# A transformer block pair on one core: the first self-attention stores its outputs by feature, and the dense stage behind it divides them by the softmax sums

## The chip, the cores and the metric

One Trainium2 chip, one of its cores. The metric is the device time of one launch, in microseconds (us), lower is better. The engines of the core are TensorE (PE, with its weight loads as PEld), VectorE (DVE), ScalarE (ACT), GpSimd (POOL) and SyncE (SP, which here issues DMAs).

## What is computed

Two cross-attention transformer layers run in sequence over x of 8 samples x 512 tokens x 320 features, with a context of 8 x 64 tokens x 192 features. There are 20 heads of 16 features. Each layer, in float32:

```python
x = x + attn(ln(x), ln(x), q1, k1, v1) @ o1_w + o1_b     # self-attention
x = x + attn(ln(x), ctx,   q2, k2, v2) @ o2_w + o2_b     # cross-attention
x = x + (a * gelu(g)) @ ff_w2 + ff_b2                    # a, g = split(ln(x) @ ff_w1 + ff_b1)

# attn, per sample and head:
sim = q @ k.T * 16 ** -0.5
out = softmax(sim) @ v
```

The second layer also rounds q, k, v and the softmax weights to 8-bit steps. The change concerns the self-attention of the first layer and the dense stage behind it.

## The kernel before

The launch is a chain of stages, each a block of its own: all engines must have ended one before the next begins. In the first layer they are a dense stage (layer norm, q, k, v), `self_attention` (here some 250 to 700 us from the start of the span), a dense stage that projects the attention output, adds it to x, normalises and makes q2 (`dense_phase` with main "q", about 702 to 840 us), `cross_attention`, and a feed-forward stage. The second layer has the same sequence with other attention functions.

`self_attention` works in 40 rounds, one for each quad (4 heads of one sample; 5 quads a sample), with work of three quads in flight. In round n, each of 8 units j makes two tiles of natural scores of quad n+2 (`nat`, in three PSUM banks; DVE takes the row maximum of each, L1391), two transposed tiles of scores of quad n (`sT`, two double banks; ACT takes the exponentials into `probs`, L1325) and a part of the product of `probs` with the values of quad n-1 into `o_ps` (L1277). In unit 1 the row maxima of the next quad are transposed on PE (L1267), and ACT copies them (L1330). `sT` is also lent to this and to the turn of the output, so each unit waits for the bank used two steps before. The values have 32 columns a head (VCOL): 16 of v, one of ones, which makes the softmax sum, and 15 of zeros. So `o_ps` holds for 4 heads 32 rows each, by feature: 16 outputs, the sum in row 16, and zeros.

At the start of round n ACT copies `o_ps` of quad n-2 to `o_sb` (L1318). In unit 2, `turn_output` transposes it by four PE transposes into `sT` (L1287), ACT copies that to `o_turned` (L1334), DVE takes the reciprocal of its sums (L1385), POOL multiplies (L1352), and SP stores 256-byte rows of 4 x 16 outputs by token into `self_out` (L1232). SP also issues all loads, in the order of its code.

The dense stage runs its samples through a written order, `body`, the same for all engines; a step of `ahead` a works on sample b+a in round b. The steps of the attention output are `oT` (transpose 128 columns of `attn_nat` on PE, L848; ACT rounds it to `oT_hi`, L949; DVE makes the rest `oT_lo`, L1012), and `oproj` (8 matmuls, L326, then DVE adds to x, L1016). `stats` is the layer norm's statistics (L1023 to L1028, POOL's power at L804), `norm` is z (L1034), `zT` its transpose with two ACT passes and `hT_lo` on DVE (L961, L963, L1048), and q the product that is stored as a high and a low part (L984, L1070). SP loads `attn_nat` of sample b+3 after the last `oT` transposes of sample b+2 (L691, L695):

```python
body = [("stats", 0), *oT[0:2], items[0], oT[2], ("norm", 0), items[1], items[2], oproj[0], ("double", 0),
        zT[0], zT[1], oproj[1], zT[2], oproj[2], oproj[3]]
```

The dense stages of the second layer take their attention output by feature already (`by_feature`), and do without the transposes.

## Time and profile before

| | |
|---|---|
| time of 3 runs, us | 3338.16, 3343.64 (median), 3344.39 |
| time of the profiled execution, us | 3342.7 |
| its span, us | 3341.0 |
| mean granted TensorE clock over the span, share of full speed | 0.841 |
| busy share of the span: PE, DVE, ACT, POOL | 88%, 65%, 57%, 24% |

The busy share of PE counts matmuls from issue to their modelled end; they are pipelined, so it is not its share of peak. The shares are means over stages with different limits, so a stage that is changed has to be read by itself. A granted clock of 1.00 is 2.4 GHz, 0.50 is 1.2 GHz.

### The profile page before, as it was taken

To read this page: it belongs to the slowest core of one execution; us is meant where nothing else is said; L and a number is where in the kernel's file an instruction comes from. 1 tells how busy PE (TensorE), PEld (TensorE's weight loads), DVE (VectorE), ACT (ScalarE), POOL (GpSimd) and SP (SyncE) were. 2 spreads that over 40 slices of the span, in tenths; PEclk is the share of its full clock that TensorE was granted. 3 is DMA by queue.
4 is the path that set the end of the run, shared out by engine and by line. 5 is a ranking of instruction groups with operands and counts; after the bars stand their busy time and mean duration, and the time that the engine had idled before them with its cause. 6 is when DMAs were issued, how large, how long until landed. Compare 5 with 4: busy or idle time off the path is not lost. (4 is left out here: it accounts for less than half of the span.)

```text
span 3341.0 us, 47964 instructions
## 1 busy us (share of the span) xinstructions
PE 2936.9 (88%) x15594; PEld 1775.7 (53%) x15594; DVE 2157.7 (65%) x3834; ACT 1892.4 (57%) x3214; POOL 805.5 (24%) x1149
## 2 busy tenths in 40 slices
PE   6989999978696999998959999879978577899999
PEld 5754444457455888886731111111126342788888
DVE  5668888837453444444649999968868685444443
ACT  4328888844353232233549999989975355333322
POOL 2021221114640000000027888200003471200000
PEclk9969999989798999998975555555559898899999
DMA  8663333336762000001567557266723213010000
GB/s 228 211 166 101 106 107 103 90 80 158 165 176 46 10 10 19 9 0 38 152 173 163 128 137 164 32 90 83 97 56 96 79 45 92 26 36 18 25 17 16
DMA packets 358243, 296.57 MB, mean 89 GB/s; under 512 B 175602, under 2 KB 281914, under 8 KB 358058
## 3 DMA queue, kind: packets, MB, share of 16 engines
q1 hardware_dynamic: 347994, 273.93, 34.0%
q0 software_dynamic: 7280, 18.07, 2.1%
q10 hardware_dynamic: 2784, 2.29, 0.4%
q8 instruction: 94, 1.54, 0.2%
q14 instruction: 91, 0.75, 0.1%
HBM read 177.53 MB, written 114.52 MB: 87 GB/s over the span
## 5 line engine op out<-in xcount | busy, mean ns | idle before, releaser
L1591 PE MATMUL nat<-k_stack,q_stack 48*128 48x512 bf16 x640 | 381.0, 605 | 71.5 <-DMA k_stack<-k1w 31.1
L1391 DVE TENSOR_REDUCE neg_max<-nat 128x1 f32<-128x512 f32 x640 | 400.7, 682 | 61.3 <-PE nat L1250 61.2
L1625 DVE TENSOR_REDUCE m_all<-nat 128x1 f32<-128x512 f32 x640 | 423.3, 691 | 18.1 <-PE nat L1591 17.8
L804 POOL TENSOR_TENSOR rstd<-var_eps,neghalf 128x4 f32<-128x4 f32 x48 | 51.9, 1081 | 1588.0 <-DVE var_eps L1028 1588.0
L1645 ACT ACTIVATE nat<-nat,m_all 128x512 f32<-128x512 f32 x640 | 427.7, 2130 | 3.0 <-DVE m_all L1625 2.9
L1645 ACT ACTIVATION_READ_ACCUMULATOR nat<-nat,m_all 128x1 f32 x640 | 403.6, 1674 | 0.0
L1054 DVE SCALAR_TENSOR_TENSOR ff<-outp,bias,gel 128x512 f32<-128x512 f32 x160 | 120.1, 751 | 417.6 <-PE outp L326 417.6
L1325 ACT ACTIVATE probs<-sT 128x1024 f32<-128x1024 f32 x320 | 328.0, 1027 | 93.1 <-PE sT L1259 85.5
L968 ACT ACTIVATE gel<-outp,bias 128x512 f32<-128x512 f32 x160 | 110.0, 688 | 351.6 <-PE outp L326 351.6
L1839 ACT ACTIVATE exps<-sT 128x1024 f32<-128x1024 f32 x320 | 293.4, 1573 | 10.5 <-PE sT L1788 10.5
L972 ACT CAST ff_hi<-ff 128x512 fp32r<-128x512 f32 x160 | 99.2, 620 | 312.3 <-DVE ff L1054 312.3
L1591 PEld LDWEIGHTS nat<-k_stack,q_stack 48*128 48x128 bf16 x640 | 64.1, 102 | 387.9 <-ACT nat L1645 350.8
L1876 DVE TENSOR_SCALAR probs<-exps 128x1024 bf16<-128x1024 f32 x320 | 218.3, 692 | 67.8 <-ACT exps L1839 67.8
L1788 PE MATMUL sT<-q_stack,k_stack 51*128 51x512 bf16 x640 | 194.2, 604 | 34.6 <-DMA q_stack<-shift_rows 12.2
L1250 PE MATMUL nat<-k_stack,q_stack 48*128 48x512 f32 x640 | 200.8, 524 | 20.1 <-DMA k_stack<-k_hi 11.7
L1277 PE MATMUL o_ps<-probs,v_stack 128*32 128x256 f32 x2560 | 199.8, 394 | 1.1 <-issue 1.1
L1057 DVE TENSOR_TENSOR ff_lo<-ff,ff_hi 128x512 fp32r<-128x512 f32 x160 | 122.1, 763 | 109.7 <-ACT ff_hi L972 109.7
L1048 DVE TENSOR_TENSOR hT_lo<-h,hT_hi 128x512 fp32r<-128x512 f32 x144 | 111.6, 780 | 106.0 <-ACT hT_hi L963 105.7
L1250 PEld LDWEIGHTS nat<-k_stack,q_stack 48*128 48x128 f32 x640 | 80.0, 193 | 163.6 <-DVE neg_max L1391 129.2
L1259 PE MATMUL sT<-q_stack,k_stack 51*128 51x512 f32 x640 | 157.7, 430 | 0.5 <-ACT probs L1325 0.2
L1788 PEld LDWEIGHTS sT<-q_stack,k_stack 51*128 51x128 bf16 x640 | 34.0, 102 | 184.0 <-ACT exps L1839 165.7
L326 PE MATMUL outp<-hT_hi,Wff_hi 128*128 128x512 f32 x320 | 125.9, 393 | 4.6 <-DVE hT_lo L1048 4.6
(561 smaller groups left out, 7163.3 us busy)
## 6 DMA issues: line engine op xcount, KB each, us to landing
v<-vpad SPq DMA_DIRECT2D x64, 320.0 KB, 2.8
q_stack<-q_part SPq DMA_DIRECT2D x90, 160.0 KB, 5.8
k_stack<-k1w SPq DMA_DIRECT2D x90, 160.0 KB, 10.5
q_stack<-q_hi SPq DMA_DIRECT2D x160, 64.0 KB, 2.5
v_stack<-v SPq DMA_DIRECT2D x40, 256.0 KB, 3.2
q_stack<-q_hi SPq DMA_DIRECT2D x80, 128.0 KB, 2.8
raw<-v SPq DMA_DIRECT2D x16, 640.0 KB, 14.9
k_stack<-k_hi SPq DMA_DIRECT2D x158, 64.0 KB, 2.2
```

The costliest lines, as they stand in the source:

```text
L326: mm = pe.matmul(out, stay, move, start=(n == 0), stop=(n == len(terms) - 1))
L1250: pe.matmul(nat[(16 * n + t) % 3][:, :], q_stack[half, n % RING, pr, qt * P:(qt + 1) * P], k_stack[half, n % RING, pr, :], start=True, sto ...
L1259: mm = pe.matmul(sT[use % 2][:, ab, :], k_stack[half, n % RING, pr, kt * P:(kt + 1) * P], q_stack[half, n % RING, pr, :], start=True, stop ...
L1277: mm = pe.matmul(o_ps[VCOL * h:VCOL * h + VCOL, tok], v_stack[:, n % 2, kt, VCOL * h:VCOL * h + VCOL], probs[:, n % 2, h, kt, tok], start= ...
L1325: act.activation(probs[:, n % 2, 2 * pr:2 * pr + 2, kt, :], sT[use % 2][:, :, :], ACT.Exp, scale=DH ** -0.5).then_inc(s["a_turn_free"], 1)
L1391: dve.tensor_reduce(neg_max[:, n % 2, qt, 2 * pr + ab:2 * pr + ab + 1], nat[(16 * (n + 2) + t) % 3][:, :], AX.X, ALU.max, negate=True).the ...
L1591: pe.matmul(bank[i % NAT][:, :], q_stack[half, slot, g, pr, qt * P:(qt + 1) * P], k_stack[half, slot, g, pr, :], start=True, stop=True).th ...
L1625: dve.tensor_reduce(k.m_all[:, column(i // TILES, i % TILES)], bank[i % NAT][:, :], AX.X, ALU.max, negate=True).then_inc(s["e_max_ready"], 1)
L1645: act.activation(b[:, :], b[:, :], ACT.Exp, bias=k.m_all[:, col], accum_out=k.s_all[:, col]).then_inc(s["a_nat_free"], 1)
L1788: mm = pe.matmul(sT[u % TURNS][:, ab, :], k_stack[half, slot, g, pr, kt * P:(kt + 1) * P], q_stack[half, slot, g, pr, :], start=True, stop ...
L1839: act.activation(exps[:, u % EXPS], sT[u % TURNS][:, :, :], ACT.Exp).then_inc(s["a_turn_free"], 1)
L1876: dve.tensor_scalar(probs[:, u % KEPT], exps[:, u % EXPS], ROUND, -ROUND, ALU.add, ALU.add).then_inc(s["e_rounded"], 1)
```

## The change

`self_attention` no longer turns its output. `o_sb` is doubled, and SP stores it as it is: 128 rows (4 heads x 32) of 512 tokens, 2 KB each, for every quad. When the five quads of a sample are stored, SP loads the 20 rows of sums back as 80 x 128 values, DVE takes one reciprocal for the sample (`invert`, in the middle of the maxima of a later round), POOL splits it into a rounded high part and the rest (`split_shares`), and SP stores both into a new scratch, `self_shares`. All of it is some rounds behind the quads; for the last sample it follows the last quad.

The dense stage loads per sample the 40 rows of shares (20 high, 20 low) and the outputs by feature (four DMAs). Its `oT` transposes go. In a new step `scale`, of the third sample ahead and late in the round, a matmul of the 40 rows with a constant 0/1 matrix (`spread`) puts the share of each head on its 16 feature rows in a bank of the old `oT` ring, and DVE multiplies `attn_T` by that bank in place, three times a sample. ACT and DVE then make `oT_hi` and `oT_lo` of the next sample from SBUF. SP loads sample b+3 when DVE has made the last `oT_lo` of sample b+2.

```diff
+            if scale:
+                ahead["scale"] = 3
             body = [("stats", 0), *oT[0:2], items[0], oT[2], ("norm", 0), items[1], items[2], oproj[0], ("double", 0),
-                    zT[0], zT[1], oproj[1], zT[2], oproj[2], oproj[3]]
+                    zT[0], zT[1], oproj[1], zT[2], *scale[0:2], oproj[2], *scale[2:], oproj[3]]
         else:
             ahead = {"stats": 1, "norm": 1, "zT": 1}
...
+                        heads = rows(attn_in, b * (QUADS * P), QUADS * P).rearrange("(h c) t -> h c t", c=VCOL)[:, 0:DH, :]
+                        loads = [(attn, heads)]
+                        if main == "ff":
+                            shared = rows(recips, b * HEADS, HEADS).unsqueeze(1).broadcast_to([HEADS, DH, TOK])
+                            loads.append((shares, shared))
+                        else:
+                            sp.dma_start(words(shares[:, :]), rows(recips, b * (2 * HEADS), 2 * HEADS)
+                                         ).then_inc(s["attn_in_loaded"], 16)
+                        for tile, src in loads:
+                            for c in range(2):
+                                sp.dma_start(tile[:, c, :], src[8 * c:8 * c + 8]).then_inc(s["attn_in_loaded"], 16)
+                            for half in range(2):
+                                sp.dma_start(tile[64 * half:64 * half + 64, 2, :], src[16:HEADS]
+                                             ).then_inc(s["attn_in_loaded"], 16)
+                        return
                     src = rows(attn_in, b * D, D)
...
+                    if kind == "scale" and main != "ff":
+                        if isinstance(b, int) and b + m == 0:
+                            pe.wait_ge(s["spread_set"], at["spread_set"] + 1)
+                        if m == 0:
+                            pe.wait_ge(s["attn_in_loaded"],
+                                       at["attn_in_loaded"] + b * (16 * n_attn) + 16 * n_attn)
+                        bank_free(pe, st, b)
+                        pe.matmul(bank_of(st, r)[:, :], spread[:, m * P:(m + 1) * P], shares[:, :], start=True, stop=True
+                                  ).then_inc(s[turned[st][0] + "_full"], 1)
...
-                    if kind == "oT":
+                    if kind == "scale":
+                        if m == 0:
+                            dve.wait_ge(s["attn_in_loaded"],
+                                        at["attn_in_loaded"] + b * (16 * n_attn) + 16 * n_attn)
+                        share, done = shares[:, m, :] if main == "ff" else bank_of(st, r)[:, :], "o_scaled"
+                        if main != "ff":
+                            done = turned[st][0] + "_drained"
+                            bank_full(dve, st, b)
+                        dve.tensor_tensor(attn[:, m, :], attn[:, m, :], share, ALU.mult).then_inc(s[done], 1)
...
+                def load_sums(b):
+                    for r in range(2):
+                        wait(sp, f"a_o_stored{r}", 16 * ((QUADS * (b + 1) - r + 1) // 2))
+                    sums_of = rows(out, b * (QUADS * P), QUADS * P).rearrange("(h c) t -> h c t", c=VCOL)[:, DH, :]
+                    sp.dma_start(sums[:, :], sums_of.rearrange("h (x t) -> h x t", t=P)
+                                 ).then_inc(s["a_sums_loaded"], 16)
+
+                def store_shares(b):
+                    wait(sp, "a_share_split", 2 * b + 2)
+                    for i, half in enumerate((share_hi, share_lo)):
+                        sp.dma_start(rows(recips, (2 * b + i) * HEADS, HEADS).rearrange("h (x t) -> h x t", t=P),
+                                     words(half[:, :])).then_inc(s["a_recip_stored"], 16)
...
                         load(n + AHEAD, k_stack, kk, (0, 1, 0))
-                    if exists(n - 3):
-                        wait(sp, "a_o_normed", n - 2)
-                        sp.dma_start(rows(out, (n - 3) * TOK, TOK).rearrange("(t p) c -> p t c", p=P),
-                                     o_nat[:, (n - 3) % 2].rearrange("p t h c -> p t (h c)")
-                                     ).then_inc(s[f"a_o_stored{(n - 3) % 2}"], 16)
+                    if exists(n - 2):
+                        wait(sp, "a_o_copied", n - 1)
+                        sp.dma_start(rows(out, (n - 2) * P, P), o_sb[:, n % 2, :]).then_inc(s[f"a_o_stored{n % 2}"], 16)
+                    if exists(n - 3) and (n - 3) % QUADS == QUADS - 1:
+                        load_sums((n - 3) // QUADS)
+                    if exists(n - 6) and (n - 6) % QUADS == QUADS - 1:
+                        store_shares((n - 6) // QUADS)
...
-                def turn_output(n):
-                    wait(pe, "a_o_copied", n + 1)
-                    wait(pe, "a_turn_free", output_use(n) - 1)
-                    for qt in range(TT):
-                        mm = pe.transpose(output_bank(n)[:, qt * P:(qt + 1) * P], o_sb[:, qt * P:(qt + 1) * P],
-                                          k.ident[:, :])
-                    mm.then_inc(s["a_turn_full"], 1)
 
...
-                        if exists(n - 2) and j == 2:
-                            turn_output(n - 2)
                         for i in PRODUCTS.get(j, ()) if exists(n - 1) else ():
...
-                        wait(act, "a_turn_full", output_use(n - 3) + 1 if n > 2 else 0)
-                        act.copy(o_sb[:, :], o_ps[:, :]).then_inc(s["a_o_copied"], 1)
+                        wait(act, f"a_o_stored{n % 2}", 16 * (n // 2 - 1))
+                        act.copy(o_sb[:, n % 2, :], o_ps[:, :]).then_inc(s["a_o_copied"], 1)
                     for j in range(UNITS):
...
-                        if exists(n - 2) and j == 2:
-                            wait(act, "a_turn_full", output_use(n - 2) + 1)
-                            wait(act, "a_o_normed", n - 3)
-                            act.copy(o_turned[:, n % 2, :], output_bank(n - 2)).then_inc(s["a_turn_free"], 1)
...
+                def split_shares(b):
+                    wait(pool, "a_recip", b + 1)
+                    wait(pool, "a_recip_stored", 32 * b)
+                    pool.tensor_copy(share_hi[:, :], shares[:, :]).then_inc(s["a_share_split"], 1)
+                    wait(pool, "a_share_split", 2 * b + 1)
+                    pool.tensor_tensor(share_lo[:, :], shares[:, :], share_hi[:, :].bitcast(F32), ALU.subtract
+                                       ).then_inc(s["a_share_split"], 1)
...
-                    if n >= 4:
-                        norm(n - 4)
+                    if n > 2 * QUADS and n % QUADS == 1:
+                        split_shares(n // QUADS - 2)
...
-                for n in range(-2, NQ + 3):
-                    if exists(n - 3):
-                        wait(dve, "a_turn_free", output_use(n - 3) + 1)
-                        wait(dve, "a_o_normed", n - 4)
-                        o = o_turned[:, (n - 3) % 2, :].rearrange("p (t h c) -> p t h c", t=TT, h=4)
-                        dve.reciprocal(recip[:, (n - 3) % 2], o[:, :, :, DH]).then_inc(s["a_recip"], 1)
+                def invert(b):
+                    wait(dve, "a_sums_loaded", 16 * (b + 1))
+                    wait(dve, "a_share_split", 2 * b)
+                    dve.reciprocal(shares[:, :], sums[:, :]).then_inc(s["a_recip"], 1)
+
+                for n in range(-2, NQ + 4):
+                    if not exists(n + 2) and exists(n - 4) and (n - 4) % QUADS == QUADS - 1:
+                        invert((n - 4) // QUADS)
...
+                        if t == 8 and exists(n - 4) and (n - 4) % QUADS == QUADS - 1:
+                            invert((n - 4) // QUADS)
...
-                        next_weights=[w1])
+                        next_weights=[w1], by_feature=True, recips=self_shares)
```

Two places in the order of instructions. First PE in `self_attention`, units 1 to 3 of one round. Before, with the line numbers of the kernel before (`o_ps` x4 are the products of one step of quad n-1; `nat` and `sT` are the score tiles):

```order
L1250 MATMUL nat_174<-k_stack,q_stack 128x512
L1250 MATMUL nat_172<-k_stack,q_stack 128x512
L1259 MATMUL sT_175<-q_stack,k_stack 128x512 x2
L1267 MATMUL sT_176<-identb,parts 32x128 x4
L1277 MATMUL o_ps<-probs,v_stack 32x256 x4
L1250 MATMUL nat_173<-k_stack,q_stack 128x512
L1250 MATMUL nat_174<-k_stack,q_stack 128x512
L1259 MATMUL sT_175<-q_stack,k_stack 128x512 x2
L1287 MATMUL sT_176<-ident,o_sb 128x128 x4
L1277 MATMUL o_ps<-probs,v_stack 32x256 x4
L1250 MATMUL nat_172<-k_stack,q_stack 128x512
L1250 MATMUL nat_173<-k_stack,q_stack 128x512
```

The same place in the changed kernel:

```order
L1314 MATMUL nat_176<-k_stack,q_stack 128x512
L1314 MATMUL nat_177<-k_stack,q_stack 128x512
L1323 MATMUL sT_179<-q_stack,k_stack 128x512 x2
L1331 MATMUL sT_178<-identb,parts 32x128 x4
L1341 MATMUL o_ps<-probs,v_stack 32x256 x4
L1314 MATMUL nat_175<-k_stack,q_stack 128x512
L1314 MATMUL nat_176<-k_stack,q_stack 128x512
L1323 MATMUL sT_179<-q_stack,k_stack 128x512 x2
L1341 MATMUL o_ps<-probs,v_stack 32x256 x4
L1314 MATMUL nat_177<-k_stack,q_stack 128x512
L1314 MATMUL nat_175<-k_stack,q_stack 128x512
```

The four transposes of `o_sb` are gone, and the two `sT` banks simply alternate from there on.

Second, DVE in the dense stage at the end of a round, from the second `oproj` on (the register rows compute what a semaphore is compared with). Before:

```order
L1016 TENSOR_TENSOR x_resid<-x_resid,oproj_225 128x320
L1047 REGISTER_ALU
L1048 TENSOR_TENSOR hT_lo<-h_214,hT_hi 128x512
L635 REGISTER_ALU
L1016 ISA
L1016 TENSOR_TENSOR x_resid<-x_resid,oproj_224 128x320
L635 REGISTER_ALU
L1016 ISA
L1016 TENSOR_TENSOR x_resid<-x_resid,oproj_225 128x320
L115 REGISTER_ALU
L1023 BN_STATS bn<-x_resid 128x6 x4
```

In the changed kernel, from the last `hT_lo` on:

```order
L1104 TENSOR_TENSOR hT_lo<-h_219,hT_hi 128x512
L1056 ISA
L644 ISA
L1062 TENSOR_TENSOR attn_T<-attn_T,oT_234 128x512
L644 REGISTER_ALU
L1062 TENSOR_TENSOR attn_T<-attn_T,oT_233 128x512
L644 REGISTER_ALU
L1072 ISA
L1072 TENSOR_TENSOR x_resid<-x_resid,oproj_229 128x320
L644 REGISTER_ALU
L1062 TENSOR_TENSOR attn_T<-attn_T,oT_234 128x512
```

Three multiplications have come in ahead of the last two additions to x, and so ahead of the next statistics.

## Rows read from the trace of the kernel before

**Rows 1.** The page's first line: the span.
```profile
span 3341.0 us, 47964 instructions
```

**Rows 2.** Windows: stretch, its length, busy us (x instructions) by engine, clock, DMA.
```profile
260.00:690.00 430.00, 417.64 (x3857) 175.39 (x3856) 359.83 (x606) 353.58 (x409) 79.87 (x210) 1.00 0.36 99
740.00:800.00 60.00, 52.57 (x312) 43.44 (x310) 47.60 (x103) 30.77 (x51) 25.87 (x35) 1.00 0.70 173
2540.00:2600.00 60.00, 55.07 (x305) 43.69 (x304) 52.11 (x110) 35.39 (x57) 20.46 (x9) 1.00 0.34 107
```

**Rows 3.** Timeline of one self-attention round: start, duration, engine, line, work, [idle before].
```profile
464.33 0.50 PE L1250 MATMUL nat<-k_stack,q_stack 48*128 48x512 f32 x2
...
465.19 0.42 PEld L1287 LDWEIGHTS sT<-ident,o_sb 128*128 128x128 f32 x4 [0.33 <-issue]
...
465.78 0.64 PE L1277 MATMUL o_ps<-probs,v_stack 128*32 128x256 f32 x8
...
466.35 0.50 PE L1250 MATMUL nat<-k_stack,q_stack 48*128 48x512 f32 x2
...
466.88 2.51 DVE L1391 TENSOR_REDUCE neg_max<-nat 128x1 f32<-128x512 f32 x4 [0.72 <-PE nat L1250]
...
467.58 0.56 PE L1250 MATMUL nat<-k_stack,q_stack 48*128 48x512 f32 x2
```

**Rows 4.** Copies and reciprocals of the self-attention: counts, durations (ns), first and last start.
```profile
L1318 ACT COPY o_sb<-o_ps x40: 578/580/586, 253.6 to 696.4; 128x512 f32<-128x512 f32 x40
L1385 DVE RECIPROCAL recip<-o_turned x40: 242/244/255, 265.2 to 698.4; 128x16 f32<-128x16 f32 x40
```

**Rows 5.** Timeline of ACT, second and third copy of the rounds.
```profile
265.19 0.58 ACT L1318 COPY o_sb<-o_ps 128x512 f32<-128x512 f32 x1
...
276.76 0.58 ACT L1318 COPY o_sb<-o_ps 128x512 f32<-128x512 f32 x1
```

**Rows 6.** Timeline of SP's queue, the end of one round.
```profile
470.68 0.42 SPq L1232 DMA_DIRECT2D self_out<-o_nat  x1
473.19 0.39 SPq L1237 DMA_DIRECT2D v_stack<-v  x1
```

**Rows 7.** Timeline between the two stages.
```profile
696.41 0.59 ACT L1318 COPY o_sb<-o_ps 128x512 f32<-128x512 f32 x1 [2.60 <-PE o_ps L1277]
...
698.75 0.62 POOL L1352 TENSOR_TENSOR o_nat<-o_turned,recip 128x256 f32<-128x256 f32 x1 [3.90 <-issue]
701.84 2.09 SPq L691 DMA_DIRECT2D attn_nat<-self_out  x4
...
707.40 1.57 PEld L848 LDWEIGHTS oT<-ident,attn_nat 128*128 128x128 f32 x8 [9.93 <-DMA attn_nat<-self_out]
```

**Rows 8.** DMAs that write or read o_nat, from issue to landing.
```profile
DMA to landing us min/median/max: 2.0/2.1/4.1
```

**Rows 9.** Timeline of one dense round: DVE, and SP's load.
```profile
766.12 1.68 DVE L1023 BATCH_NORM_STATS2 bn<-x_resid 128x6 f32 x4 [0.26 <-DVE x_resid L1016]
...
768.49 1.29 DVE L1012 TENSOR_TENSOR oT_lo<-oT,oT_hi 128x512 fp32r<-128x512 f32 x2
...
770.08 3.01 SPq L691 DMA_DIRECT2D attn_nat<-self_out  x4
...
771.15 2.66 DVE L1034 TENSOR_SCALAR z<-x_resid,mv,rstd 128x320 f32 x4
...
776.79 0.69 DVE L1048 TENSOR_TENSOR hT_lo<-h,hT_hi 128x512 fp32r<-128x512 f32 x1 [1.39 <-ACT hT_hi L963]
...
779.46 0.69 DVE L1048 TENSOR_TENSOR hT_lo<-h,hT_hi 128x512 fp32r<-128x512 f32 x1 [0.25 <-ACT hT_hi L963]
...
781.50 0.89 DVE L1023 BATCH_NORM_STATS2 bn<-x_resid 128x6 f32 x2
```

**Rows 10.** The second layer's dense stage of the same kind, by feature: DVE.
```profile
2553.05 1.51 DVE L1034 TENSOR_SCALAR z<-x_resid,mv,rstd 128x320 f32 x4
...
2556.94 2.43 DVE L1048 TENSOR_TENSOR hT_lo<-h,hT_hi 128x512 fp32r<-128x512 f32 x2 [0.81 <-ACT hT_hi L963]
```

More of the change, by code:

```diff
@@ L523, in dense_phase @@
         has_o = wo is not None
+        scale = [("scale", m) for m in range(3)] if recips is not None else []
         oT, oproj, zT = ([(x, m) for m in range(n)] for x, n in (("oT", 3), ("oproj", TT), ("zT", 3)))
@@ L529, in dense_phase @@
         if main == "ff":
-            ahead = {"oT": 1, "oproj": 1, "stats": 1, "norm": 1, "zT": 1, "tail": -1}
-            between = [[("tail", 0)], oT[0:2], oT[2:], oproj[0:2], oproj[2:], [("stats", 0)], [("norm", 0)],
+            ahead = {"oT": 1, "oproj": 1, "stats": 1, "norm": 1, "zT": 1, "tail": -1, "scale": 1}
+            between = [[("tail", 0), *scale], oT[0:2], oT[2:], oproj[0:2], oproj[2:], [("stats", 0)], [("norm", 0)],
                        zT[0:2], zT[2:], []]
@@ L551, in dense_phase @@
                 turned = {st: x for st, x in turned.items() if st[0] != "oT"}
+                turned.update({st: ("oT", st[1], 3) for st in scale})
             if not has_o:
@@ L940, in step @@
                             bank_full(act, st, b)
+                        elif scale and main == "ff":
+                            act.wait_ge(s["o_scaled"], at["o_scaled"] + b * 3 + m + 1)
+                        elif scale:
+                            name, count = bank_read(scale[m], b)
+                            act.wait_ge(s[name], count)
                         elif m == 0:
@@ L1220, in _ @@
                 load(1, k_stack, kk, (0, 1, 0))
-                for n in range(-2, NQ + 3):
+                for n in range(-2, NQ + 6):
                     if exists(n + AHEAD):
@@ L1239, in _ @@
                                      ).then_inc(s[f"a_v_loaded{(n + 1) % 2}"], 16)
-                for r in range(2):
-                    wait(sp, f"a_o_stored{r}", 16 * (NQ // 2))
+                wait(sp, "a_recip_stored", 32 * BATCH)
             @block.tensor
```

61 lines of the change are left out of this document (31 added, 30 removed).

## The prediction

> **What bounds the kernel now.** I read the page first. The span is 3341.0 us [rows 1], but its stages have different limits, so I cut it with the view of windows at the two stages that the change touches. In the self-attention PE is busy 417.6 of 430 us, DVE 359.8, ACT 353.6, at a granted clock of 1.00 [rows 2]. PE is the bound there, with DVE not far behind. In the dense stage behind it PE is busy 52.6 of 60 us and DVE 47.6 [rows 2]: near each other, so what a round costs has to be read from the order of the work.
>
> The timeline of one self-attention round shows what the removed turn costs. The two score tiles of unit 2 start at 464.33, the transposes' weight loads at 465.19, the products behind them at 465.78, and the tiles of unit 3 at 466.35; unit 3, which has no turn, ends at 467.58 [rows 3]. So unit 2 takes 2.02 us and unit 3 takes 1.23. DVE stands idle 0.72 us in that place, waiting for PE [rows 3].
>
> In the dense stage the reader is to follow DVE round the loop. From one `bn` (766.12) to the next (781.50) is 15.38 us. The first half goes to the end of z (771.15 + 2.66 = 773.81), 7.69 us, in which DVE has hardly a gap. In the second half, also 7.69 us, it waits for ACT's two passes over each `zT` tile: `hT_lo` of the first tile comes at 776.79 after 1.39 us idle, that of the third at 779.46 [rows 9].
>
> **The self-attention, round by round.** Off PE go four transposes a quad. From the first weight load of them to the next products is 0.59 us (465.78 - 465.19), the least that this saves. Unit 2 less unit 3 is 0.79 us, the most. DVE can follow by its idle 0.72. I take 0.62, near the lower end: part of the difference of the units is that the transposed scores of unit 2 wait for exponentials, and that wait stays. Rounds with a turn at the full pace are 38 (the last two quads are turned when no new scores are made), so 38 x 0.62 = 23.6 us; the bounds are 22.4 and 30.0. In the last full round of products one more turn goes, 0.6.
>
> ACT loses a copy a round (0.58 us, by the other copy of that shape [rows 4]) and POOL a product; neither is the bound, I count nothing. DVE loses a reciprocal of 0.24 us a quad [rows 4]. The trace has a round without it, because the first quad's reciprocal came only at 265.2: from the copy at 253.6 to that at 265.19 is 11.6 us, and the next, with a reciprocal, is 11.57 [rows 4, 5]. So it is worth nothing, and the eight larger ones that come in (one a sample, set in the middle of the maxima, where PE's longest unit leaves DVE a gap) I count at nothing too; uncovered they would be 8 x 0.3 = 2.4.
>
> SP's queue: the store of 256-byte rows becomes one of 2 KB rows, 0.42 us to issue as before, I assume; one quad in five adds a load, one in five two stores, 0.4 each. After its store SP is done at 471.10 and issues the values at 473.19, when the products have ended: 2.1 us of slack a round [rows 6]. A round that is 0.62 shorter and has up to 0.8 more to issue still leaves 0.7. The new waits on SP are for things some rounds old, except `a_o_copied`, which is signalled at the start of the same round, ahead of the shift that SP has waited for already.
>
> **Between the stages.** Before, the last copy of `o_ps` starts at 696.41 and the next stage's first load at 701.84, 5.4 us later [rows 7]. Now behind that copy stand, one after another: the copy with its signal 0.7, the store to its landing 2.1 [rows 8], the load of the sums 2.3 (an estimate from the same row), a reciprocal 0.4, two POOL operations 0.4 each (between nothing and the 0.62 of [rows 7], for half the elements a partition) with 0.2 between, two stores 0.4 + 2.1, the block's end 0.3. That is 9.3, and with 0.1 for each of four hand-overs 9.7: +4.2 us, between +3 and +6.
>
> **The dense stage, round by round.** Off PE go 12 transposes a sample, and three matmuls come in. DVE gets three products of 128x512 out of PSUM, which the trace does not show as such. The nearest row is the pair of `oT_lo`, one operand in PSUM, 1.29 us for two of 0.69, so 0.60 from one to the next [rows 9]. 0.69 if nothing overlaps is the upper end; nothing excludes that ACT's waits hide them, so zero is the lower.
>
> Where do they lie? They stand behind the last `hT_lo`, ahead of the last two additions to x, and the next `bn` waits for those. First half of a round: 7.5 (7.69 less the small gap before the third `oT_lo`, which waited for a transpose). Second half: in this stage the first `hT_lo` comes 2.98 us after z's end, in the second layer's, which has no transposes, 2.38 (2556.94 - 2554.56) [rows 9, 10], because PE is not late for `zT`; I take 2.38. The third comes 2.67 later, at 5.05, then 0.60 of it, then 3 x 0.60 of products, then what now stands between the third `hT_lo` and `bn` (781.50 - 779.46 - 0.60 = 1.44): 8.9. Sum 16.4, against 15.38: +1.0 us. Six rounds have both a `scale` and a whole second half: +6. Two rounds at the end have no `scale` any more and win 0.8 each: -1.6. In the opening of the stage the first loads take as long as now (5.6 us from issue to use [rows 7]), but those of sample 1 start only when DVE has split sample 0, and its `scale` stands on PE ahead of `oproj` 2 and 3 of sample 0. Two of four projections lie in between, so PE waits for a part of the 5.6; I put 1.2, between nothing and all of it. Together +5.6, between 0 (the products hidden) and +14 (all 24 at 0.69 uncovered, 16.6, less what the transposes gave).
>
> One rule speaks against this. The row: at 1.00 the second layer's stage, which lacks the transposes, has PE busy 55 of 60 us [rows 2], and the clock holds. There DVE had no products to do, here PE will idle about 1.5 us more a round, waiting for a bank that DVE must drain. The Trainium skill, "TensorE: Matmul & The Clock Gate", section on how the oscillation bites in real kernels, says that gaps in PE's work that are too long throttle the clock again, and each return of work starts cold. By the rows the stage costs +5.6, by the rule it would cost what the fourth rival says. I go by the rows: the gaps stay near those that PE has there already.
>
> **Sum.** -23.6 - 0.6 + 4.2 + 5.6 = -14.4. The profiled execution took 3342.7, 0.9 less than the median of the three, so it would become 3328.3, and the median about 3329.
>
> **Rivals.**
> (1) The dense stage costs more: each `scale` waits for its loads. SP issued the loads of a sample at 770.08 [rows 9], and will now issue them after DVE's last `oT_lo` of the round, 1.2 us later. From first issue to use takes 5.6 us [rows 7], so they are there at 776.9, 3.1 us after z's end; PE comes to `scale` at about that time (behind the third `zT`), and DVE needs its result at 5.65 after z, so they should be in time; with the queue full of stores, or DVE stretched by POOL's weight splitting, they are not. With +2 a round the stage costs +14 to +16, and the sum is -5: 3338, no change that can be told. Or DVE sets the pace of the self-attention and half the saving is lost, to much the same time. 0.16.
> (2) The self-attention wins more, because the copy to `o_turned` no longer holds a bank and unit 3 need not wait: the upper bound of 0.72 to 0.79 a round, -27 to -30, sum about -20: 3323. For it is DVE's gap at just that place; against it that PE had other work to issue. 0.13.
> (3) The other side, slower: PE's clock falls to 0.50 in the dense stage. 60 us of it hold 52.6 of PE's work [rows 2], 13.5 a round; at half the clock that is at least 20 us against the 15.4 of a round, 8 x 5 = 40 us instead of 5.6: +20, 3363. It decides from about five of the eight rounds at the low level. Against it: 1.00 in both windows of such stages. 0.06.
> (4) The change does not do what it says: the turn was hidden behind DVE, and only the tail and the stage's extra work are left, +10: 3353. Against it: DVE is idle 0.72 us at that place, for PE. 0.03.
>
> **Numbers.** The forecast has 0.62. A measurement of this kernel tells 0.2% (6.7 us) from no change. Below 3337 lie the forecast and rival 2 (0.75), with a small part of the first rival; within 3337 to 3350 most of it: faster 0.77, same 0.15, slower 0.08. The range goes from rival 2 with a dense stage at +2 (3317) to rival 1 (3340).
>
> **What will show it.** The copies `o_sb<-o_ps` should stand 10.95 us apart instead of 11.57; DVE's gap in front of unit 3's maxima should be about 0.1. From the last such copy to the next stage's first load should be 9.7 us. In the dense stage `bn` to `bn` should be 16.4, with three products behind the third `hT_lo` and no wait on `attn_T`'s loads, at a clock of 1.00. I am wrong if rounds of the self-attention are over 11.3, if `scale` waits for a DMA, or if the clock is below 1.00 between 730 and 800 us.

## The result and the profile after

The changed kernel takes 3384.6 us (median; 3381.6 to 3387.5) against 3343.7 for the kernel before on the same chip: ratio 1.0126, 95% interval 1.0109 to 1.0144. It is slower by 41 us, where a time some 15 us shorter was forecast.

The page's first line, against [rows 1]:

```profile
span 3383.2 us, 47241 instructions
```

Windows of the two changed stages, the columns as in [rows 2]:

```profile
260.00:660.00 400.00, 389.85 (x3654) 158.27 (x3651) 361.90 (x573) 331.92 (x369) 61.28 (x186) 1.00 0.41 121
740.00:800.00 60.00, 45.26 (x180) 34.91 (x179) 36.93 (x72) 20.81 (x34) 15.24 (x19) 0.78 0.38 121
```

In the self-attention DVE's busy share has risen from 84% to 90% and PE stays at 97%: the rounds are closer packed. In the dense stage no engine is full. PE falls from 52.6 to 45.3 us of 60, DVE from 47.6 to 36.9, and the granted clock from 1.00 to 0.78. So nothing is overloaded there; something is late.

Copies and reciprocals of the self-attention (counts, ns, first and last start), which answer to [rows 4]:

```profile
L1372 ACT COPY o_sb<-o_ps x40: 578/581/585, 252.5 to 668.7; 128x512 f32<-128x512 f32 x40
L1432 DVE RECIPROCAL shares<-sums x8: 937/939/949, 324.0 to 673.8; 80x128 f32<-80x128 f32 x8
```

The 40 copies now take 416.2 us from first to last, before 442.8: -26.6. The part of the change that was meant to help does help.

Then the timeline between the stages, as [rows 7]:

```profile
668.68 0.58 ACT L1372 COPY o_sb<-o_ps 128x512 f32<-128x512 f32 x1 [3.82 <-PE o_ps L1341]
669.29 0.35 SPq L1295 DMA_DIRECT2D self_out<-o_sb  x1
671.37 0.86 SPq L1269 DMA_DIRECT2D sums<-self_out  x1
673.77 0.95 DVE L1432 RECIPROCAL shares<-sums 80x128 f32<-80x128 f32 x1 [26.32 <-DMA sums<-self_out]
...
675.63 0.32 SPq L1275 DMA_DIRECT2D self_shares<-share_hi  x1
...
678.08 0.31 SPq L692 DMA_DIRECT2D shares<-self_shares  x1
...
686.75 0.76 PE L885 MATMUL oT<-shares,spread 40*128 40x512 f32 x1 [18.13 <-DMA attn_T<-self_out]
```

Read down, these are the steps of the hand-over: the store of the last outputs, the load of their sums, the reciprocal, the stores of the shares (of the two only the first is shown), and the next stage's loads. From the last copy to the next stage's first load is 9.40 us, before 5.43. And the first use of a load comes at 686.75, 8.7 us after its first issue, before 5.6.

The timeline of one dense round, the places that answer to [rows 9]: DVE's `bn` at both ends, SP's loads, and PE's `scale` with what it waited for:

```profile
752.70 1.67 DVE L1079 BATCH_NORM_STATS2 bn<-x_resid 128x6 f32 x4 [0.15 <-DVE x_resid L1072]
...
756.85 0.93 DVE L1068 TENSOR_TENSOR oT_lo<-attn_T,oT_hi 128x512 fp32r<-128x512 f32 x1
...
757.71 3.08 DVE L1090 TENSOR_SCALAR z<-x_resid,mv,rstd 128x320 f32 x4
757.98 0.34 SPq L692 DMA_DIRECT2D shares<-self_shares  x1
758.50 1.58 SPq L696 DMA_DIRECT2D attn_T<-self_out  x2
...
760.28 1.22 SPq L698 DMA_DIRECT2D attn_T<-self_out  x2
...
765.84 0.69 DVE L1104 TENSOR_TENSOR hT_lo<-h,hT_hi 128x512 fp32r<-128x512 f32 x1 [0.25 <-ACT hT_hi L1002]
767.86 1.21 PE L885 MATMUL oT<-shares,spread 40*128 40x512 f32 x2 [4.02 <-DMA attn_T<-self_out]
...
772.16 0.63 PE L326 MATMUL oproj<-o_w_hi,oT_hi 128*128 128x320 f32 x1
...
775.57 1.67 DVE L1079 BATCH_NORM_STATS2 bn<-x_resid 128x6 f32 x4 [0.26 <-DVE x_resid L1072]
```

The round is 22.87 us long, before 15.38. PE stands idle 4.02 us before `scale`, waiting for the load of a sample, whose first DMA was issued at 757.98; it is used 9.9 us later. DVE, which has made its third `hT_lo`, waits for PE. What happens to the clock in that place is in the windows around it:

```profile
764.00:766.00 2.00, 0.00 (x0) 0.00 (x0) 1.25 (x3) 1.80 (x3) 0.00 (x0) 1.00 1.02 347
766.00:768.00 2.00, 0.14 (x1) 0.14 (x1) 0.53 (x1) 0.00 (x0) 0.00 (x0) 0.74 0.68 199
768.00:770.00 2.00, 2.00 (x6) 1.35 (x7) 1.28 (x2) 0.00 (x0) 0.00 (x0) 0.50 0.28 103
```

PE does nothing from 763.8 to 767.9, the granted clock goes from 1.00 (2.4 GHz) to 0.50 (1.2 GHz), and the two projections that are left in the round run at the low level.

The time, piece by piece, from `bn` to `bn` and the copies: the last copy comes 27.7 us earlier (696.4, 668.7; 1.1 of it was there at the first copy, before the change acts); the hand-over costs +4.0; from the stage's first load to its first `bn` is 30.35 us, before 18.52, +11.8; the seven rounds to the last `bn` take 150.8 us (708.43 to 859.27), before 107.4 (720.36 to 827.73), +43.5. So the last `bn` comes 31.5 us later. The two profiled spans differ by 42.2; the other 10.7 come behind that `bn`, nearly all of it in code that is the same.

### The profile page after: what moved, and what is told of

Its sections match the earlier page's. It is cut to its first block and busy times, and to the rows that moved or that the text cites. A ratio compares the mean times of both kernels' runs of the same rounds, so it can differ in the third digit from the quotient of the medians.

```text
span 3383.2 us, 47241 instructions
## 1 busy us (share of the span) xinstructions
PE 2946.7 (87%) x15362; PEld 1776.8 (53%) x15362; DVE 2183.2 (65%) x3828; ACT 1873.0 (55%) x3174; POOL 789.4 (23%) x1125
```

## Experiments

The prediction's fear was a load that is late (its first rival) and a clock that falls (its third). Both are in the trace. The first four kernels ask how much each is worth, and whether the self-attention's part is as good alone. Each ratio below is to the kernel before, measured beside the experiment: 3341.9 us with the first four kernels, 3339.2 with the next four, 3344.5 with the last two. "Round" means from one sample's first `bn` to the next's.

**The self-attention's part alone.**

```diff
-            dense_phase(..., self_out, stores={"q": q20}, next_weights=[w1], by_feature=True, recips=self_shares)
+            by_token = self_out.rearrange("r (a c) -> (r a) c", c=4 * DH)[0:NQ * TOK, :]
+            dense_phase(..., by_token, stores={"q": q20}, next_weights=[w1])
```

> Only the self-attention part of the change; the dense stage is the one of before, run on a view of the stored rows, so its numbers are not the reference's (the sums are not divided out), and the shares are made and stored but not used. Theory A (all of the loss is in the dense stage: loads that come too late for a step that stands in order on PE, and PE's clock that falls in that wait): the self-attention and the hand-over give 27 - 4 = 23 us, median about 3320, clock in the dense stage near 0.96 to 1.00 as before. Theory B (the self-attention part also costs something later, since cross-attention was 6 us and a stage of the second layer 3 us longer in the changed kernel): 3325 to 3332. Theory C (the new self-attention disturbs the dense stage itself through memory traffic): over 3340.

3324.7 us, ratio 0.9941 (0.9919 to 0.9964): -0.59%, 20 us (the two medians themselves differ by 17). Its rounds in the dense stage are as before (from 709.51 to 801.97 six of them, 15.4 each), and its last `bn` (801.97) comes 25.8 us earlier than before, where that of the changed kernel comes 31.5 later. So what went wrong up to that point is in the dense stage.

The prediction's own terms for this part (-24.2 and +4.2) say -20.0. That they meet the 20 is partly luck. In the trace the copies win 26.8 (250.4 to 666.4) and the hand-over costs 4.0, 3.2 were there at the first copy (which starts at 249.6 to 254.0 over the twelve traces, without relation to the edits), and 7.7 of the 25.8 are lost again behind the last `bn`: the span is only 18.1 us shorter (3322.9). The time lies between theory A's 3320 and the 3325 at which theory B begins, so a loss in later, unchanged code is real in this trace; more on it below.

**Loads a round earlier.** Two tiles for outputs and shares, SP's loop unrolled:

```diff
-            attn = sb("attn_T", [P, 3, TOK])
+            attn = sb("attn_T2", [P, 2, 3, TOK])
...
-                        sp.wait_ge(s["oT_split"], at["oT_split"] + split_b * 3 + 3)
+                        if b >= 2:
+                            sp.wait_ge(s["oT_split"], at["oT_split"] + (b - 2) * 3 + 3)
```

> The changed kernel with two tiles for the loaded outputs and shares instead of one, so that a sample's loads are issued a round earlier, behind the stores of the round before; order of the steps unchanged. Theory A: no wait of PE for attn_T, clock 1.00 in the stage, rounds of 16.4 to 17 us instead of 23, dense stage about 40 us shorter, median about 3337 to 3342. Theory D (PE has too little work in this stage and the clock would fall anyway): the wait goes, but the clock stays at 0.75 to 0.9 and rounds stay over 19 us, median over 3358. Theory E (the loads are slow in themselves and PE still waits): no change from 3384.

3340.6 us, ratio 0.9992 (0.9979 to 1.0004), no change that can be told from the kernel before. As theory A expected, PE waits for the load once, 18.3 us at the opening, and not in the rounds; the clock is 1.00 from 720 to 800, and the rounds are 17.2 us long:

```profile
734.84 1.67 DVE L1090 BATCH_NORM_STATS2 bn<-x_resid 128x6 f32 x4
...
752.10 1.67 DVE L1090 BATCH_NORM_STATS2 bn<-x_resid 128x6 f32 x4 [0.26 <-DVE x_resid L1083]
```

**The clock held up, the load still late.** 24 matmuls without use, into the bank that `scale` then overwrites, ahead of its wait:

```diff
                         bank_free(pe, st, b)
                         if m == 0:
+                            for _ in range(0 if isinstance(b, int) and b == 0 else 24):
+                                pe.matmul(bank_of(st, r)[:, 0:D], wo.hi[:, 0, 0:P], ws[0].hi[:, 0, 0:D], start=True, stop=True)
                             pe.wait_ge(s["attn_in_loaded"],
```

> The changed kernel with 24 idle matmuls of 320 columns on PE ahead of each sample's first scale step (but the first), written to the bank that the scale matmul then overwrites; the loads stay as late as they are. Theory A with half of the loss from the clock: the wait for the load stays (PE now busy in it), the clock holds at 1.00, the two projections and the q product behind it run at full speed, rounds of about 20 instead of 23 us, median 3362 to 3368. If the clock costs nothing by itself (the wait is all): the same as the changed kernel, 3384. If 24 matmuls are too many: a little of it lost.

3363.2 us, ratio 1.0061 (1.0037 to 1.0085). The timeline of PE around `scale`, and the window of the stage:

```profile
759.53 3.76 PE L884 MATMUL oT<-q_hi,o_w_hi 128*128 128x320 f32 x24
763.93 0.73 PE L887 MATMUL oT<-shares,spread 40*128 40x512 f32 x2 [0.63 <-DMA attn_T<-self_out]
```

```profile
740.00:800.00 60.00, 51.26 (x285) 41.34 (x284) 44.49 (x87) 23.45 (x40) 21.90 (x27) 1.00 0.43 132
```

PE is kept busy to within 0.6 to 1.0 us of the load, and the clock stays at 1.00. Nothing useful was added, and a round is 20.1 us instead of 22.9, as expected. The load is as slow as before (first issue to use 10.0 us, 753.91 to 763.93); what is shorter is the time from `scale` to the next `bn`, 4.8 us instead of 7.7. So of the 7.5 us that a round has become longer, the low clock is 2.8, the late load itself 2.9 (20.1 to 17.2, what the version with two tiles has), and 1.8 is neither (17.2 to the 15.4 of before).

**Two tiles, and `scale` in the gaps.** The 1.8 us come where three products of DVE stand in a row behind its last `hT_lo`. With the load a round earlier they can go elsewhere:

```diff
-                    zT[0], zT[1], oproj[1], zT[2], *scale[0:2], oproj[2], *scale[2:], oproj[3]]
+                    *scale[0:1], zT[0], *scale[1:2], zT[1], oproj[1], zT[2], oproj[2], *scale[2:], oproj[3]]
```

> As the kernel with two tiles, and the three scale steps of a sample moved to where DVE waited for ACT: one ahead of zT 0, one between zT 0 and zT 1, the third behind oproj 2. Theory A: DVE's products fall into gaps of 1.4 and 0.65 us, rounds of about 15.7, 0.7 to 1 us less than with two tiles alone, median about 3330 to 3336, below the kernel before. Theory D: the clock is below 0.95 in the stage here too, median over 3350.

3332.7 us, ratio 0.9972 (0.9959 to 0.9985). The rounds are back at 15.4 us (`bn` at 735.70, 751.20, 766.63, 782.03), with the products in them, at a clock of 1.00. DVE is busy 56.7 of 60 us there, against 47.6 before.

**Why is the load late?** It takes 8.7 us from first issue to use in the opening, when nothing else runs. The windows of that place say how (share of the 16 DMA engines, GB/s at the end of each row):

```profile
679.00:681.00 2.00, 0.00 (x0) 0.00 (x0) 0.00 (x0) 0.00 (x0) 0.00 (x0) 0.50 0.39 116
681.00:683.00 2.00, 0.00 (x0) 0.00 (x0) 0.00 (x0) 0.00 (x0) 0.00 (x0) 0.50 0.47 169
683.00:685.00 2.00, 0.00 (x0) 0.00 (x0) 0.00 (x0) 0.00 (x0) 0.00 (x0) 0.50 0.35 104
```

At most half of the DMA engines' time is used, for 6 us on end. The outputs are loaded by four DMAs, over 8, 8, 4 and 4 heads, with 16 rows of each head. The next kernel loads as many bytes as contiguous rows, 256 rows in one DMA and 64 in each of two. They are not the right rows; only the time is meant:

```diff
-                        heads = rows(attn_in, b * (QUADS * P), QUADS * P).rearrange("(h c) t -> h c t", c=VCOL)[:, 0:DH, :]
+                        src = rows(attn_in, b * (2 * D), D)
...
-                            for c in range(2):
-                                sp.dma_start(tile[:, c, :], src[8 * c:8 * c + 8]).then_inc(s["attn_in_loaded"], 16)
+                        sp.dma_start(tile[:, 0:2, :], src[0:2 * P].rearrange("(c p) t -> p c t", p=P)
+                                     ).then_inc(s["attn_in_loaded"], 16)
```

> The changed kernel with one edit: the dense stage's loads of the outputs take contiguous rows (320 rows of a sample, one DMA of 256 rows and two of 64) instead of the 16 of every 32 rows that each head has. The bytes are the same 768 KB, but what is loaded is not the outputs, so the results differ; only the time is meant. Theory A: the load is slow by itself, because a DMA over 8 or 4 heads of 16 rows uses at most half of the 16 DMA engines (in the opening of the changed stage, with nothing beside it, the DMA share is 0.28 to 0.50 for 6 us, and the first use comes 9 us after the first issue). Then first issue to use falls to some 5 to 6 us, the wait of PE in a round from 4 us to under 0.5, the clock stays at 1.00, rounds go from 22.9 to about 17.2 us as with two tiles, the opening loses 4 to 8 us: about 3340. Theory B: the load is slow because it shares the queue with the stores of q right behind it. Then nothing changes: 3380 to 3387.

3339.4 us, ratio 0.9999 (0.9984 to 1.0015). The same stretch of the opening, and the `scale` of two rounds:

```profile
679.00:681.00 2.00, 0.00 (x0) 0.00 (x0) 0.00 (x0) 0.00 (x0) 0.00 (x0) 0.50 0.95 330
681.00:683.00 2.00, 0.19 (x1) 0.22 (x2) 0.00 (x0) 0.00 (x0) 0.00 (x0) 0.50 0.34 47
```

```profile
728.28 0.74 PE L880 MATMUL oT<-shares,spread 40*128 40x512 f32 x2 [1.30 <-DMA attn_T<-self_out]
744.70 0.73 PE L880 MATMUL oT<-shares,spread 40*128 40x512 f32 x2 [0.56 <-DMA attn_T<-self_out]
```

The share is 0.95 at 330 GB/s where it was 0.39 at 116. The first use comes 5.4 us after the first issue in the opening (677.36 to 682.81) and 6.4 in a round (738.27 to 744.70), PE waits 0.6 to 1.4 us in the rounds, the clock is 1.00 from 720 to 800, and the rounds are 17.2 us, all with one tile and with the steps where the change put them. Between the two ratios (this one and the 1.0126 of the changed kernel) lie 1.27%, 42 us, for a different access pattern. One DMA fewer is issued too, which accounts for a part: SP has issued the loads 2.9 us after it began in the changed kernel (678.08 to 680.99) and 2.0 us here (677.36 to 679.37), so up to 0.9 of the 3.2 us won in the opening.

The DMA engines did as much work in both kernels: summed over 2 us windows from 677, the share comes to 3.1 us of all engines by heads (0.08, 0.39, 0.47, 0.35, 0.27) and to 3.1 by rows (0.23, 0.95, 0.34, 0.04). By heads it was spread over twice the time.

The Trainium skill, "DMA: Bandwidth & Descriptors", section "Why a DMA increments its semaphore by 16 and not by 1", states the rule: the number of DMA engines is the largest up to 16 that divides the slowest dimension of both sides, and they are the lowest-numbered ones. By it the four loads use 8, 8, 4 and 4 engines, all of them among the first eight; each of the first four would carry 128 of the 768 KB, and as an estimate at 330/16/0.95 = 21.7 GB/s an engine that takes 6.0 us. The trace agrees: 6 us at a share of at most 0.5. Which engines were busy no view here shows. The shapes in the program give this before any run.

**The place of the wait.** The changed kernel with the steps at the end of the round:

```diff
-                    zT[0], zT[1], oproj[1], zT[2], *scale[0:2], oproj[2], *scale[2:], oproj[3]]
+                    zT[0], zT[1], oproj[1], zT[2], oproj[2], oproj[3], *scale]
```

> The changed kernel with one edit: the three scale steps stand behind the last projection instead of around the third, so that PE has all its work of the round issued before it waits for the load. If the place of the wait in PE's order is what matters (theory C), the projections no longer wait and the statistics of the next sample neither: rounds of 18 us or less, 3350 or less. If the late load is what matters and the place is only a part (theories A and B), PE's wait shrinks by what two projections take at full clock, 2.4 us of 4, the clock falls for less time, and rounds go from 22.9 to about 20: 3365.

3347.9 us, ratio 1.0024 (1.0014 to 1.0034), a good deal better than the 3365 expected, and within what theory C, that the place of the wait matters, named for it. With the load as slow as before, the place alone gives back 1.02% between the ratios, 34 of the 42 us. PE waits for the load in four of the six rounds that have a `scale`, 0.6 to 1.4 us (and 2.4 in the opening), the clock from 740 to 800 is 0.91, and the rounds are 17.3 to 18.9. The step of the expectation that failed is the size of the wait and with it the clock's: it still falls to 0.50 behind the wait at 718 and the one at 755, but in the round between them it stays at 1.00:

```profile
736.00:738.00 2.00, 1.90 (x10) 1.47 (x10) 1.44 (x4) 0.26 (x1) 0.00 (x0) 1.00 0.41 120
738.00:740.00 2.00, 1.36 (x5) 0.84 (x5) 2.00 (x5) 1.11 (x2) 0.00 (x0) 1.00 0.11 42
...
756.00:758.00 2.00, 1.46 (x3) 1.01 (x4) 1.92 (x4) 1.14 (x2) 0.00 (x0) 0.71 0.22 85
758.00:760.00 2.00, 2.00 (x6) 1.52 (x6) 1.85 (x8) 0.00 (x0) 0.00 (x0) 0.50 0.00 0
```

**Packed stores, four DMAs a quad.** The two-tile version with contiguous loads that are right, because the self-attention stores only the 16 rows of each head:

```diff
-                        sp.dma_start(rows(out, (n - 2) * P, P), o_sb[:, n % 2, :]).then_inc(s[f"a_o_stored{n % 2}"], 16)
+                        for h in range(4):
+                            sp.dma_start(rows(out, base + (4 * g + h) * DH, DH), o_sb[VCOL * h:VCOL * h + DH, n % 2, :]
+                                         ).then_inc(s[f"a_o_stored{n % 2}"], 16)
+                        sp.dma_start(rows(out, base + D + 4 * g, 4), o_sb[DH:P:VCOL, n % 2, :]
+                                     ).then_inc(s[f"a_o_stored{n % 2}"], 16)
```

> The version with two tiles and the scale steps in the gaps, and besides the self-attention stores only 16 rows a head, packed (four DMAs of 16 partitions a quad, and one for the four sums), so that the dense stage loads contiguous rows. Theory A: the first load takes 4 us less, 3329. If SP's four more DMAs a quad delay its loads, the self-attention's rounds get longer than 10.90: +0.3 a round would give 3341.

3376.6 us, ratio 1.0107 (1.0085 to 1.0128), where 3329, or 3341 with longer rounds, was expected. The dense stage does as wished (rounds of 15.4), but the self-attention takes 465.7 us from first to last copy (251.3 to 717.0) instead of 416.2. SP's queue at 480 to 490 us:

```profile
482.54 0.88 SPq L1252 DMA_DIRECT2D k_stack<-k_hi  x2
483.47 0.89 SPq L1252 DMA_DIRECT2D k_stack<-k_lo  x2
484.40 0.89 SPq L1252 DMA_DIRECT2D k_stack<-k_hi  x2
485.33 1.81 SPq L1303 DMA_DIRECT2D self_out<-o_sb  x4
487.18 0.55 SPq L1305 DMA_DIRECT2D self_out<-o_sb  x1
```

SP issues without a pause: the stores of a quad now take 2.4 us of its time instead of 0.4, which uses up the 2.1 us of slack a round that the prediction read from [rows 6]. PE then waits 19.6 us in all for the loads of `shift_sb`, which SP issues late; in the changed kernel it does not wait for them. A round grows by 1.3 us on average (49.5 over 39), and not by the 0.3 of the expectation.

**Stores out of the way.** The changed kernel; SP holds the stores of q back until the loads have landed:

```diff
                 def store_sample(b):
+                    if recips is not None:
+                        nxt = min(b + 3, BATCH - 1) if isinstance(b, int) else b + 3
+                        sp.wait_ge(s["attn_in_loaded"], at["attn_in_loaded"] + nxt * (16 * n_attn) + 16 * n_attn)
```

> The changed kernel with one wait more: SP issues the stores of q of a sample only when the loads of the attention output for the third sample ahead have landed. Theory B (the stores collide with the loads): first issue to use falls from 9.9 to 5 or 6 us, PE's wait to under 1 us, 3350 or less. Theory A (the loads are slow by themselves): first issue to use 8.5 to 9 us, rounds shorter by at most 1 us, 3378 to 3387.

3372.9 us, ratio 1.0099 (1.0082 to 1.0116). First issue to use goes from 9.9 to 9.4 us (757.36 to 766.72), PE's waits in the rounds are 3.3 to 4.6, and while SP's loads run, before the stores of q, the share is low again:

```profile
762.00:764.00 2.00, 1.22 (x8) 0.72 (x7) 0.81 (x2) 2.00 (x4) 0.02 (x1) 1.00 0.41 143
764.00:766.00 2.00, 0.00 (x0) 0.00 (x0) 1.67 (x3) 1.19 (x2) 0.00 (x0) 1.00 0.24 89
```

The expectation's theory A holds in kind: the loads are slow by themselves, and the collision with the stores is small, 0.5 us of this load's 9.9. In size it is missed by a little: the time is 5 us under the 3378 that theory A gave as its lowest, with rounds of 21.8 to 22.5 us (the last with a `scale` 20.6).

**Packing in one DMA a sample, with one tile and with two.** SP copies the 16 rows of each head of a sample together, from scratch to scratch, and the dense stage loads them as contiguous rows, now the right ones:

```diff
                     sp.dma_start(sums[:, :], sums_of.rearrange("h (x t) -> h x t", t=P)
                                  ).then_inc(s["a_sums_loaded"], 16)
+                    heads = rows(out, b * (QUADS * P), QUADS * P).rearrange("(h c) t -> h c t", c=VCOL)[:, 0:DH, :]
+                    sp.dma_start(rows(out, NQ * P + b * D, D).rearrange("(h c) t -> h c t", c=DH), heads
+                                 ).then_inc(s["a_packed"], 16)
```

> The changed kernel with the contiguous load made legitimate: behind the load of a sample's sums SP issues one more DMA that packs the sample's 20 x 16 rows of outputs, from the scratch to the scratch, into 320 contiguous rows, and the dense stage loads those. One DMA a sample more on SP, beside the chain of the sums, so the self-attention should stay at 10.90 us a copy and the hand-over at 9.4. Theory A: rounds of 17.2 us without a wait for the load, as with wrong rows; 3336 to 3340. If the copy of the last sample lands late, up to 2 us more in the opening. Under theory B, 3370 or more.

3344.1 us against 3344.5 for the kernel before beside it, ratio 0.9999 (0.9987 to 1.0010), where 3336 to 3340 was expected. The rounds are 17.2 us but for one of 20.6. In that one PE waited 1.86 us for the load, and the granted clock fell to 0.50 behind it; waits of up to 1.3 us in the kernel with contiguous rows had left it at 1.00 from 720 to 800:

```profile
726.00:728.00 2.00, 0.41 (x4) 0.17 (x2) 1.36 (x3) 2.00 (x4) 0.00 (x0) 1.00 1.05 374
728.00:730.00 2.00, 1.73 (x4) 1.08 (x5) 1.75 (x4) 0.38 (x1) 0.00 (x0) 0.57 0.76 284
730.00:732.00 2.00, 2.00 (x9) 1.67 (x7) 0.38 (x1) 0.00 (x0) 0.00 (x0) 0.50 0.04 16
```

The longer rounds, the opening and the hand-over together eat up what the self-attention wins.

With two tiles and `scale` in the gaps besides:

> The packed load together with two tiles and the scale steps in the gaps of the round: rounds of 15.4 us as in the version with two tiles and gaps, and an opening 3 us shorter than there, because the first load is as short as it was before the change: 3329 to 3331, against the 3332.7 measured for that version, if the last sample's packing is hidden behind the chain of its sums.

3327.8 us against 3344.5, ratio 0.9946 (0.9929 to 0.9964), a little under the 3329 to 3331 expected. This is faster than both kernels: by 17 us than the one before, and by some 60 (1.8% between the ratios) than the changed one. Its copies go from 252.9 to 671.9, 2.8 us more than in the changed kernel, and the hand-over is 10.4, 1.0 more: the packing is not quite hidden. But the rounds are 15.4, and from the first load to the first `bn` it is 21.3 us, with the loads by head 24.2:

```profile
735.12 1.67 DVE L1085 BATCH_NORM_STATS2 bn<-x_resid 128x6 f32 x4 [0.15 <-DVE x_resid L1078]
...
742.55 0.50 PE L892 MATMUL oT<-shares,spread 40*128 40x512 f32 x1
...
743.92 0.50 PE L892 MATMUL oT<-shares,spread 40*128 40x512 f32 x1
...
744.72 0.67 DVE L1068 TENSOR_TENSOR attn_T<-attn_T,oT 128x512 f32<-128x512 f32 x1
...
746.20 0.68 DVE L1068 TENSOR_TENSOR attn_T<-attn_T,oT 128x512 f32<-128x512 f32 x1
```

The products stand apart, and no `scale` waits for a DMA.

## Why the prediction was wrong

**The self-attention: right.** A round is 10.90 us (471.31 to 482.20) where 10.95 was forecast, 11.57 before [rows 5]. One round in five is 11.18, the one with the new reciprocal. That reciprocal takes 0.94 us; the forecast counted it at nothing, and 0.3 if uncovered. The eight rounds lose 0.28 each, 2.2 us. In all the copies win 26.6 against the 24.2 forecast, inside its bounds. DVE's gap before unit 3 did not go to 0.1: gaps of 0.35 to 0.43 remain, so PE was again the one waited for. The kernel with this part alone confirms the size (26.8).

**Between the stages: right.** 9.4 us, forecast 9.7. The reciprocal was too small in the sum, and the other steps a little too large.

**The dense stage: the term of +5.6 was mis-sized, and the stage cost +55.** The step that failed is "From first issue to use takes 5.6 us [rows 7], so they are there at 776.9", in the first rival; the forecast's opening uses the same 5.6. It took the time of [rows 7] for another shape of DMA. Those rows are of DMAs over 128 partitions of tokens; the new ones are over 8 and 4 heads. From first issue to use they take 8.7 us alone and 9.9 in a round, which is the whole slack and 4 us more. The mechanism was named, its price was put at 2 us a round, and the chance at 0.16. The kernel with contiguous rows shows it: with them the load takes 5.4 us alone and 6.4 in a round, PE waits at most 1.4 us, and the 1.0 us a round that the forecast put on this stage is 1.8.

Of the 0.8 that are more than forecast, 0.6 is in the first half of the round, 8.1 us and not 7.5: z takes 3.08 us for 2.66 in [rows 9], and the third `oT_lo` 0.93 for 0.69. z takes 3.08 to 3.09 in the traces of the new dense stage and 2.67 in the one with the self-attention's part alone. The cause was not tried; POOL's splitting of weights runs beside z in the kernel before as well (771.45 to 775.66), so it is not enough by itself. The second half is 9.1 to 9.2 with the contiguous rows, forecast 8.9.

The second step that failed is "the gaps stay near those that PE has there already". With the load in time they leave the clock at 1.00. With it late PE has one gap of 4 us in each round, and the clock falls behind it (0.78 over 60 us of the stage). This is the third rival's mechanism, and the rule of the Trainium skill that I had set against the rows ("TensorE: Matmul & The Clock Gate", the section on how the oscillation bites in real kernels) is what happened, though by a wait for a load and not by the bank. (The prediction says there "what the fourth rival says"; the rival of the clock is its third.) It is worth 21 us, the difference of the changed kernel to the one with idle matmuls. The rival put +40 on the stage, because it had all eight rounds at the low level; that its sum for the whole kernel was +20 is another quantity.

**The opening: mis-sized, +11.8 for +1.2.** From first load to first `bn`, 30.35 us. The longer load is paid twice, because that of sample 1 starts when sample 0 is split, and its `scale` stands ahead of two projections of sample 0: PE waits another 5.0 us for it, at a mean clock of 0.60 between 680 and 720. With contiguous rows 22.3 us remain.

So the two rivals were not alternatives: the late load brings the low clock, which lengthens what is left of the round. Both are mended by an earlier issue or by a faster load, and mostly by putting the wait behind PE's other work; the 1.8 us a round go when the steps stand in DVE's gaps.

**Behind the stage: not in the forecast, +10.7.** Of these 5.2 us are in the cross-attention, whose code no kernel here changes. Its windows from the first copy of `o_sb` to the last, the kernel before and the changed one:

```profile
882.80:1024.30 141.50, 134.98 (x812) 76.60 (x812) 71.02 (x148) 75.47 (x113) 71.80 (x193) 0.97 0.59 151
914.80:1061.50 146.70, 142.69 (x811) 80.47 (x810) 72.09 (x148) 75.07 (x113) 71.58 (x193) 0.91 0.57 146
```

The granted clock is lower in the second. Over the twelve traces the length goes with it: 141.0 to 141.7 us where its mean is 0.96 to 0.98 (seven traces), 143.5 and 143.6 at 0.93 (stores held back; packing with one tile), 146.7 to 149.5 at 0.90 to 0.91 (the changed kernel, the self-attention's part alone, two tiles with `scale` in the gaps). One of the last has the old dense stage, and the kernel with packing and gaps is among the first, so the dense stage's edits do not decide it. Why the clock is lower there was not tried, and one trace a kernel cannot tell an effect of the kernel from a difference between executions; the trace of 149.5 is of the slowest of its kernel's ten (3341.9 us, median 3332.7). The other 5.5 us lie almost all behind the cross-attention (2321.7 us from its last copy to the end, before 2316.7) and stay open.

## What to carry to other kernels

Before taking a load's time from a row, look whether the new DMA has the same slowest dimension: a load over 8 or 4 groups took 8.7 us where one by rows took 5.4, and the windows show it as a DMA share under 0.5 while nothing else runs. When a change puts a wait for a DMA into PE's work, which runs in the order of the code, put it behind all work of the round that does not need it (34 us here), or issue the load a buffer earlier. A wait that comes every round is to be charged with the clock too: here 4 us of waiting cost 2.8 more.

## What was unexpected in the hardware

- The same 768 KB moved at 104 to 169 GB/s by heads and at 330 GB/s by rows.
- 24 idle matmuls of 3.76 us in front of a wait made the kernel 21 us faster. A wait of 1.86 us was followed by a clock of 0.50 (packing, one tile), and so was one of 0.88 us with 0.56 us more behind it (the steps at the end of the round, 755 to 758).
- A DVE reciprocal of 80x128 takes 0.94 us, and one of 128x16 0.24 [rows 4]: 6.2 ns more for each further column, against 1.3 ns a column for a maximum of 128x512 (0.68 us).
- SP spends 0.45 us on each small store; five a quad instead of one lengthened the self-attention by 49.5 us.
